# Expert slots in twos: a 64-row remainder of the down projection in two row tiles

## The chip, the cores and the metric

The kernel runs on one core of a Trainium2 chip. The metric is the device time of one execution in microseconds (us). Engines are named as the profile names them: PE is TensorE (matmuls and transposes), PEld its weight loads, DVE is VectorE, ACT is ScalarE, POOL is GpSimd, SP is SyncE, which here only issues transfers.

## The reference, cut to what matters

A cross-attention layer is followed by a mixture-of-experts feed-forward layer over 4096 tokens of width D = 256. The change touches only the routed experts. Each token goes to the 2 best of E = 8 experts, each expert having a hidden width of F = 192:

```python
h = jax.nn.silu(jnp.einsum('nd,edf->enf', xr, Wg)) * jnp.einsum('nd,edf->enf', xr, Wu)
out_all = jnp.einsum('enf,efd->end', h, Wd)
routed = out_all[exp, jnp.arange(exp.shape[0])]
out = shared.at[tok].add(routed * w[:, None])
```

All arithmetic of this part is in float32.

## The kernel before, in words

The first two thirds of the kernel compute attention, routing and the shared expert. Tokens are sorted by expert into DRAM (`sorted_rows`), in tiles of 128 rows that belong to one expert. There are 72 such tiles, called slots, and they are worked in 18 turns of four: the first turn and the last are written out, and a hardware loop (`quads`) runs the sixteen between. The number of a slot's expert is read from a table (`etile`) into a register, which then selects the weights.

For one slot, PE does the following. It transposes the 128 x 256 rows (`transposes`, L944, two slots to a call). It multiplies them with gate and up weights, 384 columns in two chunks of 128 rows (`up`, L955). ACT takes the silu of the gate half (L705), and DVE multiplies it with the up half (L1402, `inner`). PE transposes the product, 192 columns as two pieces of 96 (`turn`, L962), DVE copies it out of PSUM (L1408, `columns`), and PE does the down projection as two chunks of 96 rows and 256 columns (`down`, L971). DVE scales the result by the router's weight (L1417, `result`). POOL adds it to the output in DRAM with an indirect transfer (L530, a scatter), and it has a buffer for each of the four slots of a turn. `columns` in the ACT program (L696) copies the transposed rows of the next turn, two slots at a time.

The order of PE within a turn is written out by hand: up 0, up 1, turn 0, up 2, turn 1, down 0, up 3, turn 2, down 1, transposes of the next turn's first half, turn 3, down 2, transposes of its second half, down 3. That of DVE is: inner 0, inner 1, columns 0, inner 2, columns 1, result 0, inner 3, columns 2, result 1, columns 3, result 2, `places` of the next turn (small table operations, L1387 to L1394), result 3. Gate banks and down banks are two each, by k % 2.

POOL waits before the scatter of slot i for the scatter three before it; where a slot is the first tile of an expert it also waits until the scatter of the slot before has landed, and one further where it is among the first two, since two experts may hold the same token. These last waits use values that it loads from a table (L527).

The shared expert has the same width, 192. Its down projection (`shared_down`) runs for each pair of token tiles two matmuls over the full 128 rows (L1019) and then two over 64 rows, one in the lower half of the array and one in the upper (L1022). The helper `aside` increments a semaphore of its own.

A float32 matmul stands in the trace as two MATMUL records (and two LDWEIGHTS), a float32 transpose as one.

Of the kernel before, what the change touches and what calls it, by code (L numbers as in the profile page):

```python
# [22 lines left out]
ALU = mybir.AluOpType  # L23
# [52 lines left out]
def more(a, tiles):  # L76

    return not (isinstance(a, int) and a == tiles // 4 - 1)


def build(nc, x, xT, ctxT, wq, wkv, wp, bp, ln_g, ln_b, centre, ident, ident16, own, wr, wgu, wd, wgu_s, wd_s, e_bias, tri_c, rev_c, reg_c, tok_c, tst_c, fill_c,
          gate_c, x2_cols, sorted_rows, out):
    ctx = ExitStack()
    with ctx:
# [6 lines left out]
        def sem(name):  # L91
            return ctx.enter_context(nc.semaphore(name))

        def views(memory, *shapes):

            at, out_ = 0, []
            for shape in shapes:
                n_ = int(np.prod(shape))
                v_ = memory[:, at:at + n_]
                if len(shape) == 2:  # L100
                    v_ = v_.rearrange("p (a b) -> p a b", a=shape[0])
                if len(shape) == 3:
                    v_ = v_.rearrange("p (a b c) -> p a b c", a=shape[0], b=shape[1])
                out_.append(v_)
                at += n_
            return out_
# [70 lines left out]
        gate = gate.bitcast(I32)  # L177
        spare_at = spare_at.bitcast(I32)
        xs_col, hs0, hs1, gs0, gs1 = views(scores_in[:, :], (2, 4, D), (2, 4, P), (2, 2, P), (4, P), (4, P))
        x_col, act_g, h_in, h_col = views(scores_in[:, :], (4, D), (4, F), (2, F), (4, D))  # L180
        x_row, y_out = views(VS[:, :, :, :].rearrange("p b h d -> p (b h d)"), (4, ROW), (4, D)) if False else (
            views(VS[:, :, :, :].rearrange("p b h d -> p (b h d)"), (4, ROW))[0], VR[:, :, :, :].rearrange("p b g d -> p (b g) d").rearrange(
                "p (k q) d -> p k (q d)", k=4))
# [97 lines left out]
        f_xt, f_xc, f_gu, f_si, f_h, f_ht, f_hc, f_y, f_yd = (  # L281
            {k: sem(f"{k}_{n_}") for k in kinds_} for n_ in ("xt", "xc", "gu", "si", "h", "ht", "hc", "y", "yd"))
        e_dst = sem("e_dst")
        e_chain = sem("e_chain")
        y_st = [sem(f"y_st{i}") for i in range(4)]
        spare_set = sem("spare_set")

        def gate_bank(k):

            return bankS[:, k % 2, :]  # L290

        def down_bank(k):
            return bankS[:, 2 + k % 2, 0:D]
# [9 lines left out]
        def aside(eng):  # L303

            eng.sem_inc(aside_n[eng.engine], 1)
# [11 lines left out]
        def _(sp):  # L317
# [32 lines left out]
            sp.wait_ge(kt_rd, len(halves))  # L350
            for k in range(KC):
                sp.dma_start(wgu_sb[:, k], wgu[k * P:(k + 1) * P]).then_inc(w_in, 16)
            for k in range(FC):
                sp.dma_start(wd_sb[0:FP, k], wd[k * FP:(k + 1) * FP]).then_inc(w_in, 16)
            for m in range(LATE):
                store(m)

# [176 lines left out]
        def _(act):  # L534
# [156 lines left out]
            def columns(a):  # L691


                for h in range(2):
                    act.wait_ge(f_xt["e"], 2 * a + (h + 1))
                    act.activation(x_col[:, 2 * h:2 * h + 2], row_bank(h).rearrange("p (t c) -> p t c", t=2), ACT.Copy) \  # L696
                        .then_inc(f_xc["e"], 1)

            def ffn(kind, tiles):
                def gates(a):  # L700
                    for k in range(4):
                        act.wait_ge(f_gu[kind], 4 * a + (k + 1))
                        if not isinstance(a, int) or a >= 1:
                            act.wait_ge(f_h[kind], 4 * a + (k - 3))
                        act.activation(act_g[:, k], gate_bank(k)[:, 0:F], ACT.Silu).then_inc(f_si[kind], 1)  # L705
                    if more(a, tiles):
                        columns(a + 1)
                return gates

            def shared(a):  # L710

                act.wait_ge(s_gu, 3 * a + 1)
                if a >= 1:
                    act.wait_ge(s_h, 2 * a - 1)
                act.activation(gs0, bankS[:, 0, :], ACT.Silu).then_inc(s_si, 1)
                act.wait_ge(s_gu, 3 * a + 3)
                if a >= 1:
                    act.wait_ge(s_h, 2 * a)
                act.activation(gs1[0:P // 2], bankS[0:P // 2, 2, :], ACT.Silu).then_inc(s_si, 1)
# [8 lines left out]
            logit_exps(PARTS - 1)  # L728
            for a in range(1, QUADS):
                shared(a)  # L730
            columns(0)
            quads(act, SLOTS, ffn("e", SLOTS))

        @block.tensor
        def _(pe):
# [211 lines left out]
            def ffn(kind, tiles):  # L947
                def four(a):
                    def up(k, e_):

                        if k % 2 == 0:
                            pe.wait_ge(f_xc["e"], 2 * a + (k // 2 + 1))
                        for c in range(KC):
                            rhs = wgu_sb[:, c, ds(e_, 1), :].rearrange("p o f -> p (o f)")
                            last = pe.matmul(gate_bank(k)[:, 0:2 * F], x_col[:, k, c * P:(c + 1) * P], rhs, start=(c == 0), stop=(c == KC - 1))  # L955
                        last.then_inc(f_gu[kind], 1)

                    def turn(k):

                        pe.wait_ge(f_h[kind], 4 * a + (k + 1))  # L960
                        for c in range(FC):
                            last = pe.transpose((bankQ, bankR)[k % 2][0:FP, c * P:(c + 1) * P], h_in[:, k % 2, c * FP:(c + 1) * FP], id32[:, :])  # L962
                        last.then_inc(f_ht[kind], 1)

                    def down(k, e_):
                        pe.wait_ge(f_hc[kind], 4 * a + (k + 1))
                        if k >= 2 or not isinstance(a, int) or a >= 1:
                            pe.wait_ge(f_yd[kind], 4 * a + (k - 1))
                        for c in range(FC):
                            rhs = wd_sb[0:FP, c, ds(e_, 1), :].rearrange("p o d -> p (o d)")  # L970
                            last = pe.matmul(down_bank(k), h_col[0:FP, k, c * P:(c + 1) * P], rhs,  # L971
                                             start=(c == 0), stop=(c == FC - 1))
                        last.then_inc(f_y[kind], 1)

                    e_ = [expert(4 * a)] + [None] * 3
                    for k in range(4):
                        up(k, e_[k])
                        if k < 3:
                            e_[k + 1] = expert(4 * a + (k + 1))
                        if k >= 1:  # L980
                            turn(k - 1)
                        if k >= 2:
                            down(k - 2, e_[k - 2])
                    if more(a, tiles):
                        transposes(a + 1, 0)
                    turn(3)
                    down(2, e_[2])
                    if more(a, tiles):
                        transposes(a + 1, 1)
                    down(3, e_[3])  # L990
                return four

            pe.wait_ge(ws_in, 16 * 2)
# [50 lines left out]
            for a in range(3, QUADS):  # L1044
                shared(a)
            shared_down(QUADS - 1)
            pe.wait_ge(w_in, 16 * (KC + FC))
            pe.wait_ge(routed, 1)
            transposes(0, 0)
            transposes(0, 1)  # L1050
# [3 lines left out]
        def _(dve):  # L1054
# [341 lines left out]
            def ffn(kind, tiles):  # L1396
                def four(a):
                    def inner(k):
                        dve.wait_ge(f_si[kind], 4 * a + (k + 1))
                        if k >= 2 or not isinstance(a, int) or a >= 1:  # L1400
                            dve.wait_ge(f_ht[kind], 4 * a + (k - 1))
                        dve.tensor_tensor(h_in[:, k % 2], act_g[:, k], gate_bank(k)[:, F:2 * F], ALU.mult).then_inc(f_h[kind], 1)  # L1402

                    def columns(k):

                        dve.wait_ge(f_ht[kind], 4 * a + (k + 1))
                        aside(dve)
                        dve.tensor_copy(h_col[0:FP, k], (bankQ, bankR)[k % 2][0:FP, 0:D]).then_inc(f_hc[kind], 1)  # L1408

                    def result(k):  # L1410
                        dve.wait_ge(f_y[kind], 4 * a + (k + 1))
                        if not isinstance(a, int) or a >= 1:
                            dve.wait_ge(y_st[k], BASE + 16 * a)
                        dve.wait_ge(e_dst, 2 * a + (k // 2 + 1))
                        aside(dve)
                        w_k = w_slot[:, ds(4 * a + k, 1)]
                        dve.tensor_tensor(y_out[:, k], down_bank(k), w_k.to_broadcast([P, D]), ALU.mult).then_inc(f_yd[kind], 1)  # L1417

                    inner(0)
                    inner(1)  # L1420
                    columns(0)
                    inner(2)
                    columns(1)
                    result(0)
                    inner(3)
                    columns(2)
                    result(1)
                    columns(3)
                    result(2)
                    if more(a, tiles):  # L1430
                        places(a + 1)
                    result(3)
                return four

# [98 lines left out]
```

## Time and profile before

| | |
|---|---|
| median of 3 runs | 616.65 us (615.98 to 617.1) |
| the profiled execution's own time | 616.69 us |
| its span in the profile | 614.9 us |
| PE busy | 524.6 us, 85% of the span |
| DVE busy | 345.0 us, 56% |
| ACT busy | 239.4 us, 39% |
| POOL busy | 244.2 us, 40% |

The expert slots run from about 405 us to the end of the span. Busy shares say little on their own here, since every stage has another limit; the stage of the slots is to be read by itself, from the order of the instructions in one turn.

### The profile page before, as it was taken

What the parts mean: (1) busy time and instruction counts of PE and PEld (TensorE: products, weight loads), DVE (VectorE), ACT (ScalarE), POOL (GpSimd) and SP (SyncE); (2) the same over time, 40 slices, a digit from 0 to 9 for tenths busy, and PEclk for the clock granted to TensorE, in tenths of its full rate; (3) what the DMA queues carried; (4) which work ended last, traced back from release to release, by engine and by line L of the source; (5) the groups of instructions that cost most, each with busy time, mean ns of one, the idle gap of its engine ahead of it and who ended that gap; (6) DMA issues with size and microseconds to landing.
All of it is one profiled execution on the core that took longest, in us unless ns stands there. A gap on an engine that the chain in (4) does not pass through costs nothing.

```text
span 614.9 us, 10970 instructions
## 1 busy us (share of the span) xinstructions
PE 524.6 (85%) x2868; PEld 311.6 (51%) x2869; DVE 345.0 (56%) x1040; ACT 239.4 (39%) x468; POOL 244.2 (40%) x218
## 2 busy tenths in 40 slices
PE   4746899998798977988689999479999999999990
PEld 3633245544354444433265555157676766767670
DVE  5875556777747757635556663225555555555550
ACT  0256888776647834654324111012222222222220
POOL 5353411120011533442114475605656547564644
PEclk9956999998969967988879999879999999999996
DMA  8903701110011211121054384225656547565634
GB/s 276 354 30 132 212 18 36 45 61 18 17 36 35 88 52 53 60 80 52 19 190 150 105 275 155 91 73 80 116 84 105 99 80 118 86 110 88 103 55 48
DMA packets 41685, 59.75 MB, mean 97 GB/s; under 512 B 6703, under 2 KB 32047, under 8 KB 41168
## 3 DMA queue, kind: packets, MB, share of 16 engines
q0 software_dynamic: 16256, 26.49, 21.2%
q1 hardware_dynamic: 25392, 32.82, 17.9%
q8 instruction: 17, 0.28, 0.2%
q14 instruction: 20, 0.16, 0.1%
HBM read 31.76 MB, written 29.52 MB: 100 GB/s over the span
## 4 chain that ended last, share of the span: by engine, by line
PE 67%; DVE 13%; DMA 7%; issue 5%; ACT 4%; POOL 2%; POOLq 1%; SPq 1%; DVEq 0%; ACTq 0%
PE bankS L955 13%; PE bankS L971 8%; PE bankV L866 7%; PE bankR L741 7%; PE bankS L1006 6%; PE bankQ L741 5%; DMA out<-VR,attn 5%; PE bankV L870 3%; PE bankS L841 2%; PE bankS L853 2%; PE bankR L748 1%; ACT attn L622 1%; PE bankS L1022 1%; PE bankD L944 1%; PE bankQ L962 1%
## 5 line engine op out<-in xcount | busy, mean ns | idle before, releaser
L530 POOL DMA_INDIRECT out<-VR,attn x72 | 111.1, 1544 | 101.2 <-DVE VR L1417 57.0
L955 PE MATMUL bankS<-experts,scores_in 128*128 x288 | 105.0, 498 | 2.1 <-issue 1.1
L473 POOL DMA_INDIRECT sorted_rows<-XR,route x64 | 63.3, 989 | 107.1 <-PE bankD L872 48.6
L622 ACT ACTIVATE attn<-bankS,bias 128x512 f32<-128x512 f32 x128 | 81.1, 680 | 24.3 <-PE bankS L841 24.2
L971 PE MATMUL bankS<-experts,scores_in 96*128 x288 | 74.3, 380 | 0.0
L866 PE MATMUL bankV<-attn,VS 128*32 128x512 f32 x256 | 69.0, 664 | 1.7 <-DVE OTT L1192 1.7
L955 PEld LDWEIGHTS bankS<-experts,scores_in 128*128 128x128 f32 x288 | 52.6, 193 | 34.2 <-issue 9.7
L868 PE MATMUL bankD<-attn,ON 128*32 128x512 f32 x256 | 68.9, 664 | 0.0
L705 ACT ACTIVATE scores_in<-bankS 128x192 f32<-128x192 f32 x72 | 23.8, 330 | 110.8 <-PE bankS L955 110.8
L409 POOL DMA_DIRECT2D x_in<-in_xT x13 | 9.6, 736 | 127.3 <-PE bankQ L741 126.3
L1402 DVE TENSOR_TENSOR scores_in<-scores_in,bankS 128x192 f32<-128x192 f32 x72 | 25.5, 354 | 52.5 <-ACT scores_in L705 52.1
L971 PEld LDWEIGHTS bankS<-experts,scores_in 96*128 96x128 f32 x288 | 48.9, 190 | 4.6 <-issue 0.7
L1417 DVE TENSOR_TENSOR VR<-bankS,attn 128x256 f32<-128x256 f32 x72 | 30.6, 425 | 29.0 <-PE bankS L971 14.6
L1006 PE MATMUL bankS<-scores_in,wgus_sb 128*128 128x512 f32 x96 | 43.8, 603 | 0.0
L741 PE MATMUL bankQ<-wq_sb,x_in 128*128 128x256 f32 x112 | 35.0, 470 | 0.0
L870 PE MATMUL bankV<-attn,VR 128*32 128x512 f32 x128 | 34.7, 621 | 0.0
L872 PE MATMUL bankD<-attn,OR 128*32 128x512 f32 x128 | 34.6, 621 | 0.0
L748 PE MATMUL bankR<-id,XR 128*128 128x128 f32 x56 | 10.7, 323 | 27.3 <-DVE XR L1213 27.3
L866 PEld LDWEIGHTS bankV<-attn,VS 128*32 128x32 f32 x256 | 13.0, 117 | 39.9 <-issue 33.9
L1199 DVE TENSOR_TENSOR X<-X,bankR 128x512 f32<-128x512 f32 x14 | 9.6, 688 | 38.3 <-PE bankR L741 38.3
L741 PEld LDWEIGHTS bankQ<-wq_sb,x_in 128*128 128x128 f32 x112 | 26.0, 241 | 4.8 <-issue 0.3
L1006 PEld LDWEIGHTS bankS<-scores_in,wgus_sb 128*128 128x128 f32 x96 | 17.5, 190 | 20.7 <-issue 20.1
(252 smaller groups left out, 916.9 us busy)
## 6 DMA issues: line engine op xcount, KB each, us to landing
VS<-sorted_rows SPq DMA_DIRECT2D x72, 130.0 KB, 2.9
x_cols<-X2T SPq DMA_DIRECT2D x16, 256.0 KB, 2.0
scores_in<-x_cols SPq DMA_DIRECT2D x16, 256.0 KB, 2.8
out<-X POOLq DMA_DIRECT2D x8, 512.0 KB, 4.1
x_in<-in_xT POOLq DMA_DIRECT2D x15, 256.0 KB, 3.5
experts<-in_wgu SPq DMA_DIRECT2D x2, 1536.0 KB, 9.1
X<-in_x SPq DMA_DIRECT2D x1, 2048.0 KB, 16.2
experts<-in_wd SPq DMA_DIRECT2D x2, 768.0 KB, 15.9
```

Of the source, the lines that this page charges most:

```text
L473: pool.indirect_dma_start(sorted_rows.rearrange("s p r -> (s p) r"), bass.IndirectOffsetOnAxis(ap=index, axis=0), rows, None, bounds_check ...
L530: pool.indirect_dma_start(out, bass.IndirectOffsetOnAxis(ap=dest[:, i:i + 1], axis=0), y_out[:, i % 4], None, bounds_check=B * N + SPARE - ...
L622: act.activation(Pb[:, u % 2, c, :], bankS[:, c % GH, :], ACT.Exp, bias=bias[:, b, GH * g + c:GH * g + c + 1] if c < GH else biasR[:, b, g ...
L741: last = pe.matmul(bank[:, t * width:(t + 1) * width], columns(t, k), weights[:, k, :], start=(k == 0), stop=(k == KC - 1))
L866: pe.matmul(bankV[v_at:v_at + 32, :], VS[:, b, GH * g + 2 * c + a_, :], Pb[:, u % 2, 2 * c + a_, :], start=(a_ == 0), stop=False)
L868: pe.matmul(bankD[d_at:d_at + 32, :], ON[:, a_, :], Pb[:, u % 2, 2 * c + a_, :], start=(a_ == 0), stop=False)
L870: pe.matmul(bankV[v_at:v_at + 32, :], VR[:, b, g, 32 * c:32 * c + 32], Pb[:, u % 2, GH, :], start=False, stop=True)
L872: last = pe.matmul(bankD[d_at:d_at + 32, :], ones_r[:, 32 * c:32 * c + 32], Pb[:, u % 2, GH, :], start=False, stop=True)
L955: last = pe.matmul(gate_bank(k)[:, 0:2 * F], x_col[:, k, c * P:(c + 1) * P], rhs, start=(c == 0), stop=(c == KC - 1))
L971: last = pe.matmul(down_bank(k), h_col[0:FP, k, c * P:(c + 1) * P], rhs, start=(c == 0), stop=(c == FC - 1))
L1006: last = pe.matmul(bankS[:, c, :], wgus_sb[:, k, c * P:(c + 1) * P], xs_col[:, a % 2, :, k * P:(k + 1) * P], start=(k == 0), stop=(k == KC ...
L1417: dve.tensor_tensor(y_out[:, k], down_bank(k), w_k.to_broadcast([P, D]), ALU.mult).then_inc(f_yd[kind], 1)
```

## The change

Slots are worked in twos, h = 0 and 1 in a turn. The product of a pair is transposed in three pieces of 128 columns in place of four of 96: the first 128 hidden columns of either slot, and a third piece that holds the last 64 of both. For that DVE writes the product of an odd slot with its two parts exchanged, in two multiplications (64 and 128 columns) in place of one. One copy of 128 x 384 then takes the place of two of 96 x 256. `down` works a pair: two matmuls over 128 rows, one for each slot, and then two over 64 rows, one slot in the lower half of the array and the other in the upper. The 64 weight rows of the remainder are loaded twice, once for either half of the partitions, and as the two experts may differ, ACT copies each slot's 64 x 256 weights into `wd_rest`, with a load of the expert number ahead of each copy. The orders of PE and DVE within a turn are new, as the diff shows.

```diff
+            sp.dma_start(wd_sb[:, 0], wd[0:P]).then_inc(w_in, 16)
+            for r in range(2):
+                sp.dma_start(wd_sb[r * P // 2:(r + 1) * P // 2, 1], wd[P:F]).then_inc(w_in, 16)
...
+            def rest_weights(a, k):
+                h, rows = k // 2, slice(P // 2 * (k % 2), P // 2 * (k % 2) + P // 2)
+                if not isinstance(a, int) or a >= 1:
+                    act.wait_ge(f_y["e"], 2 * a + (h - 1))
+                    aside(act)
+                e_ = act.value_load(etile[0:1, ds(4 * a + k, 1)], min_val=0, max_val=E - 1)
+                act.activation(wd_rest[rows, h], wd_sb[rows, 1, ds(e_, 1), :].rearrange("p o d -> p (o d)"), ACT.Copy).then_inc(f_wr, 1)
...
                         act.activation(act_g[:, k], gate_bank(k)[:, 0:F], ACT.Silu).then_inc(f_si[kind], 1)
+                        rest_weights(a, k)
...
+                    def turn(h):
+                        bank = (bankQ, bankR)[h]
+                        pe.wait_ge(f_h[kind], 4 * a + (2 * h + 2))
+                        for t in range(2):
+                            pe.transpose(bank[:, t * P:(t + 1) * P], h_in[:, h, 2 * P * t:2 * P * t + P], id32[:, :])
+                        pe.transpose(bank[:, 2 * P:3 * P], h_in[:, h, P:2 * P], id32[:, :]).then_inc(f_ht[kind], 1)
+
+                    def down(h, e_):
+                        half = P // 2
+                        pe.wait_ge(f_hc[kind], 2 * a + (h + 1))
+                        pe.wait_ge(f_wr, 4 * a + (2 * h + 2))
+                        if h >= 1 or not isinstance(a, int) or a >= 1:
+                            pe.wait_ge(f_yd[kind], 4 * a + 2 * h)
+                        for t in range(2):
+                            rhs = wd_sb[:, 0, ds(e_[t], 1), :].rearrange("p o d -> p (o d)")
+                            pe.matmul(down_bank(t), h_col[:, h, t * P:(t + 1) * P], rhs, start=True, stop=False)
+                        for t in range(2):
+                            rows = slice(half * t, half * t + half)
+                            last = pe.matmul(down_bank(t), h_col[rows, h, 2 * P:3 * P], wd_rest[rows, h], start=False, stop=True)
                         last.then_inc(f_y[kind], 1)
...
                     for k in range(4):
+                        if k >= 2:
+                            pe.wait_ge(f_h[kind], 4 * a + (k - 1))
                         up(k, e_[k])
                         if k < 3:
                             e_[k + 1] = expert(4 * a + (k + 1))
-                        if k >= 1:
-                            turn(k - 1)
-                        if k >= 2:
-                            down(k - 2, e_[k - 2])
+                        if k == 2:
+                            turn(0)
+                    down(0, e_[0:2])
                     if more(a, tiles):
                         transposes(a + 1, 0)
-                    turn(3)
-                    down(2, e_[2])
+                    turn(1)
                     if more(a, tiles):
                         transposes(a + 1, 1)
-                    down(3, e_[3])
+                    down(1, e_[2:4])
...
+                        if k % 2 == 0:
+                            last = dve.tensor_tensor(h_in[:, k // 2, 0:F], act_g[:, k], gate_bank(k)[:, F:2 * F], ALU.mult)
+                        else:
+                            dve.tensor_tensor(h_in[:, k // 2, F:2 * P], act_g[:, k, P:F], gate_bank(k)[:, F + P:2 * F], ALU.mult)
+                            last = dve.tensor_tensor(h_in[:, k // 2, 2 * P:2 * F], act_g[:, k, 0:P], gate_bank(k)[:, F:F + P], ALU.mult)
...
+                        dve.tensor_copy(h_col[:, h], (bankQ, bankR)[h][:, 0:2 * F]).then_inc(f_hc[kind], 1)
...
                     inner(1)
                     columns(0)
                     inner(2)
+                    inner(3)
+                    result(0)
+                    result(1)
                     columns(1)
-                    result(0)
-                    inner(3)
-                    columns(2)
-                    result(1)
-                    columns(3)
-                    result(2)
                     if more(a, tiles):
                         places(a + 1)
+                    result(2)
                     result(3)
```

## Rows read from the trace of the kernel before

**Rows 1.** Busy time by stretch (windows): turns 0 to 13, turns 14 to 17; busy PE, PEld, DVE, ACT, POOL, clock
```profile
405.50:558.20 152.70, 150.81 (x673) 105.19 (x672) 80.84 (x301) 35.80 (x85) 81.98 (x54) 0.99 0.57 94
558.20:600.30 42.10, 41.80 (x184) 28.95 (x184) 22.19 (x83) 8.87 (x22) 22.91 (x15) 1.00 0.56 85
```

**Rows 2.** Timeline of PE, turn 5: start us, length us, engine, line, count
```profile
460.71 2.84 PE L955 MATMUL bankS<-experts,scores_in 128*128 x8
463.39 0.38 PE L962 MATMUL bankQ<-id,scores_in 128*96 128x128 f32 x2
463.61 1.46 PE L955 MATMUL bankS<-experts,scores_in 128*128 x4
...
469.02 1.03 PE L971 MATMUL bankS<-experts,scores_in 96*128 x4
469.89 0.60 PE L944 MATMUL bankD<-id,VS 128*128 128x128 f32 x4
470.32 1.03 PE L971 MATMUL bankS<-experts,scores_in 96*128 x4
471.44 0.58 PE L955 MATMUL bankS<-experts,scores_in 128*128 x1
```

**Rows 3.** Timeline of the shared expert's down projection, 364.7 to 370.5 us
```profile
365.23 0.59 PE L1019 MATMUL bankQ<-wds_sb,scores_in 128*128 128x256 f32 x2
...
365.75 0.48 PE L1022 MATMUL bankS<-wds_sb,scores_in 64*128 64x256 f32 x1
...
365.76 0.48 PE L1022 MATMUL bankQ<-wds_sb,scores_in 64*128 64x256 f32 x1
...
366.08 0.38 PE L1022 MATMUL bankQ<-wds_sb,scores_in 64*128 64x256 f32 x1
366.38 0.30 PEld L1019 LDWEIGHTS bankS<-wds_sb,scores_in 128*128 128x128 f32 x2 [0.33 <-issue]
...
367.44 0.48 PE L1022 MATMUL bankS<-wds_sb,scores_in 64*128 64x256 f32 x1
```

**Rows 4.** Groups by shape: busy us, mean ns of one, idle before
```profile
L1449 DVE TENSOR_TENSOR scores_in<-scores_in,bankS 128x512 f32<-128x512 f32 x8 | 5.5, 688 | 6.7 <-PE bankS L1006 5.4 <-ACT scores_in L715 1.2
L1408 DVE COPY scores_in<-bankQ 96x256 f32<-96x256 f32 x36 | 14.8, 412 | 0.0
L556 ACT ACTIVATE qs<-nq 128x512 f16<-128x512 f32 x16 | 10.1, 629 | 3.5 <-DVE nq L1118 3.5
```

**Rows 5.** Timeline from a product to its transpose (turn 9), and of a result (turn 14)
```profile
505.95 0.35 DVE L1402 TENSOR_TENSOR scores_in<-scores_in,bankS 128x192 f32<-128x192 f32 x1 [0.46 <-ACT scores_in L705]
506.36 0.28 PEld L962 LDWEIGHTS bankQ<-id,scores_in 128*96 128x96 f32 x2 [0.30 <-DVE scores_in L1402]
506.51 0.38 PE L962 MATMUL bankQ<-id,scores_in 128*96 128x128 f32 x2
...
562.63 1.03 PE L971 MATMUL bankS<-experts,scores_in 96*128 x4
562.69 0.33 ACT L705 ACTIVATE scores_in<-bankS 128x192 f32<-128x192 f32 x1 [1.18 <-PE bankS L955]
...
564.12 0.43 DVE L1417 TENSOR_TENSOR VR<-bankS,attn 128x256 f32<-128x256 f32 x1 [0.38 <-issue]
```

**Rows 6.** Timeline of POOL: slots 63, 64, 65 and 71
```profile
583.80 1.54 POOL L530 DMA_INDIRECT out<-VR,attn  x1 [0.63 <-DMA out<-VR,attn]
589.24 1.54 POOL L530 DMA_INDIRECT out<-VR,attn  x1 [3.90 <-issue]
594.47 1.54 POOL L530 DMA_INDIRECT out<-VR,attn  x1 [3.68 <-issue]
...
607.59 1.54 POOL L530 DMA_INDIRECT out<-VR,attn  x1 [0.67 <-issue]
```

**Rows 7.** The chain that ended last: one register load of POOL
```profile
593.08 0.29 POOLq L527
```

**Rows 8.** Timeline of PE: the start of turn 15
```profile
568.95 1.23 PE L955 MATMUL bankS<-experts,scores_in 128*128 x3
```

More of the change, by code:

```diff
@@ L179, in build @@
         xs_col, hs0, hs1, gs0, gs1 = views(scores_in[:, :], (2, 4, D), (2, 4, P), (2, 2, P), (4, P), (4, P))
-        x_col, act_g, h_in, h_col = views(scores_in[:, :], (4, D), (4, F), (2, F), (4, D))
+        x_col, act_g, h_in, h_col, wd_rest = views(scores_in[:, :], (4, D), (4, F), (2, 2 * F), (2, 2 * F), (2, D))
         x_row, y_out = views(VS[:, :, :, :].rearrange("p b h d -> p (b h d)"), (4, ROW), (4, D)) if False else (
@@ L283, in build @@
         e_dst = sem("e_dst")
+        f_wr = sem("f_wr")
         e_chain = sem("e_chain")
@@ L352, in _ @@
                 sp.dma_start(wgu_sb[:, k], wgu[k * P:(k + 1) * P]).then_inc(w_in, 16)
-            for k in range(FC):
-                sp.dma_start(wd_sb[0:FP, k], wd[k * FP:(k + 1) * FP]).then_inc(w_in, 16)
+            sp.dma_start(wd_sb[:, 0], wd[0:P]).then_inc(w_in, 16)
+            for r in range(2):
+                sp.dma_start(wd_sb[r * P // 2:(r + 1) * P // 2, 1], wd[P:F]).then_inc(w_in, 16)
             for m in range(LATE):
@@ L730, in _ @@
                 shared(a)
+            act.wait_ge(routed, 1)
+            act.wait_ge(w_in, 16 * (KC + 3))
             columns(0)
@@ L956, in up @@
                         last.then_inc(f_gu[kind], 1)
[L958 to L972, printed above, removed]
+                    def turn(h):
[16 more added lines that the diff above has]
+                            last = pe.matmul(down_bank(t), h_col[rows, h, 2 * P:3 * P], wd_rest[rows, h], start=False, stop=True)
                         last.then_inc(f_y[kind], 1)
@@ L1046, in _ @@
             shared_down(QUADS - 1)
-            pe.wait_ge(w_in, 16 * (KC + FC))
+            pe.wait_ge(w_in, 16 * (KC + 3))
             pe.wait_ge(routed, 1)
@@ L1399, in inner, with columns @@
                         dve.wait_ge(f_si[kind], 4 * a + (k + 1))
[L1400 to L1406, printed above, removed]
+                        if not isinstance(a, int) or a >= 1:
+                            dve.wait_ge(f_ht[kind], 2 * a + (k // 2 - 1))
+                        if k % 2 == 0:
[3 more added lines that the diff above has]
+                            last = dve.tensor_tensor(h_in[:, k // 2, 2 * P:2 * F], act_g[:, k, 0:P], gate_bank(k)[:, F:F + P], ALU.mult)
+                        last.then_inc(f_h[kind], 1)
+                    def columns(h):
+                        dve.wait_ge(f_ht[kind], 2 * a + (h + 1))
                         aside(dve)
-                        dve.tensor_copy(h_col[0:FP, k], (bankQ, bankR)[k % 2][0:FP, 0:D]).then_inc(f_hc[kind], 1)
+                        dve.tensor_copy(h_col[:, h], (bankQ, bankR)[h][:, 0:2 * F]).then_inc(f_hc[kind], 1)
                     def result(k):
-                        dve.wait_ge(f_y[kind], 4 * a + (k + 1))
+                        dve.wait_ge(f_y[kind], 2 * a + (k // 2 + 1))
                         if not isinstance(a, int) or a >= 1:
```

## The prediction

> **What bounds the kernel now.** I read the busy times by stretch first. From 405.5 to 600.3 us PE is busy for all but 2.2 us of 194.8, at a granted clock of 0.99 to 1.00 (the 2.4 GHz level), while DVE and POOL are busy about half the time and ACT a quarter [rows 1]. After that PE has nothing to do and POOL scatters on. So there are two clocks to watch: PE's period per turn, and POOL's chain at the end.
>
> The timeline of a turn gives the period: 471.44 - 460.71 = 10.73 us. Starts inside it give the pieces, better than the lengths, which contain the way through the array: `up` is 8 records from 460.71 to 463.39 less the late first start, that is 1.29 us for one slot; `turn` 0.22 (463.39 to 463.61); four row transposes 0.43 to 0.44 (469.89 to 470.32), 0.109 each; one `down` 0.87 (469.02 to 469.89), 0.216 for each record [rows 2]. Sum: 4 x 1.29 + 4 x 0.865 + 4 x 0.22 + 2 x 0.44 = 10.37. The other 0.36 is the loop's own turn: the last `down` starts at 470.32 and has streamed by 471.19, and the next weight load comes only at 471.4. Everything else is back to back.
>
> At the end, slot 63 is scattered at 583.80, 14.85 us after turn 15 began (568.95) [rows 6, 8]. Slots 64 and 65 are first tiles and wait for landings (5.44 and 5.23 us after the one before), then six scatters follow every 2.19 us, up to 607.59; the span ends 7.3 us later [rows 6]. From slot 63 on, 31.1 us are POOL's and not PE's. So PE's period counts for the 15 turns ahead of turn 15 and not for the last three, unless it becomes a good deal worse: PE was done at 600.3 against the last scatter at 607.59.
>
> **The change part by part, per turn.**
>
> *Full chunks and fewer transposes.* Two pairs, each with four full records of 0.216 (0.865) and, were the row tiles free, two more lengths for the four half-height records (0.43): 2 x 1.295 = 2.59 in place of 3.46. Six transposes of 0.109 = 0.655 in place of 0.88. Ideal: 5.16 + 2.59 + 0.655 + 0.88 + 0.36 = 9.64, a gain of 1.09.
>
> *What the row tiles really cost.* The shared expert does exactly this pair. The two halves do run together (365.75 and 365.76). But the first half-height record starts 0.52 after a full one whose successor should be done after 0.43, the second pair comes 0.32 after the first, and the next full load waits until 366.38, with 0.33 us of idle before it, put down to issue. From 365.75 to the same place at 367.44 is 1.69 us, against 1.295 of streaming [rows 3]. So 0.40 is lost in each trip into the row tiles and back, 0.80 per turn. The second way back falls into the loop's 0.36, so I take 0.6; ends 0.4 and 0.8. The Trainium skill, "TensorEngine Tiling (Array Packing)", Key Properties, says that changing the tiling mode drains TensorE, and gives up to 2x for a contraction of 64 rows or less. The trace agrees with the first (the 0.40), and with the second only inside the mode; by the 2x alone the sum would have nothing in this place.
>
> *The wait in front of the second `down`.* Before, a copy of columns had a whole `down` and four transposes to hide behind (turn 3, down 2, transposes, down 3). Now turn(1) is followed by 0.44 of transposes and then by down(1), which needs columns(1). That copy stands on DVE behind result(0) and result(1), which wait for down(0). Time from down(0)'s first record: last record ends 0.96 + 0.32 + 0.38 = 1.67. A result starts 0.46 after its `down` ended (562.63 + 1.03 to 564.12 [rows 5]); I have it start at 2.05. Two results of 0.43 [rows 5] with a little overlap end at 2.87. The copy of 384 columns lies halfway between 0.412 for 256 and 0.688 for 512, the nearest DVE rows that read PSUM at those widths: 0.55 [rows 4], to 3.42. From the end of a DVE product (506.30) to the transpose that needs it (506.51) it is 0.21, weight load included [rows 5]: 3.6. PE itself is free at 1.70 + 0.44 + 0.33 + 0.44 = 2.91. Stall 0.7; with the result starting 0.15 earlier and tighter overlap 0.45. I take 0.6; ends 0.4 and 0.9. Nothing covers it: PE has no other work queued.
>
> *Others.* DVE's odd products become 64 and 128 columns: by the same slope, 1.08 ns a column, from the 0.35 of 192 [rows 5], 0.21 + 0.28, about 0.1 more than one of 192. That lies in slack: `up` 2 runs ahead of turn(0) for 1.29 us, and the product of slot 1 is ready some 1.1 us after up 1 (silu 0.33, product 0.45, hand-overs). The third product has down(0) ahead of turn(1). `up` 2 now waits for product 0 as turn(0) did, at the same moment: nothing. POOL still gets four results a turn, now in twos; it needs 4 x 2.19 = 8.8 us for them, under the period, and result 0 comes later in the turn but result 3 earlier against POOL's queue, so slot 63 stays within 0.3 us of 14.85.
>
> *ACT's copies.* 64 x 256 lies between the silu's 0.33 for 192 columns and 0.629 for 512, that is about 0.39 [rows 4, 5]. Silu 0.33, a register load (POOL's takes 0.29 [rows 7]) and copy are 1.01 of the 1.29 between two silus: hidden, as ACT idles 1.18 ahead of each. Queued behind a copy are the next silu and then the row columns of the next turn; if the load took 0.35 more, each silu would be late and turn(0) with it. Ends 0 and 0.35 per turn. Waits on f_y are for a turn ago, met long before. *The loads:* three of 1.0 MB and 2 x 0.5 MB in place of two of 0.75 MB, over 300 us before use; 0.5 MB more is about 3 us of transfer beside attention, cost nothing, at most 1. *The loop's turn:* the last gate, columns(1), now has sixteen PE instructions after it instead of eight, which can make the sequencer later at the loop's end; 0.05, ends -0.15 and 0.2.
>
> **Sum.** 9.64 + 0.6 + 0.6 + 0.05 = 10.89 us a turn against 10.73: +0.16. Fifteen turns: +2.4. Turn 5 stands for all of them: fifteen of 10.73 from turn 0's 405.5 give 566.5, and turn 15 began at 568.95 [rows 1, 8], so 2.5 us lie in the start and in single late turns, which I leave in both. 616.69 (the profiled execution; the median is 616.65) + 2.4 = 619.1.
>
> **The rivals.**
> - *Forecast, 619.1, chance 0.42.* The packing is paid back by the two trips and by the wait at down(1). Its own range is 617.9 to 623.
> - *Equal, 616.5, chance 0.23.* The same, with both terms at the low side (0.5 and 0.5): 10.69. What can be measured of this kernel is about 0.2%, 1.2 us, either way, from 615.4 to 617.9.
> - *Faster: PE's sequencer gains at the loop's turn and DVE's chain is short, 612, chance 0.17.* Down(1) leaves 1.3 us of queued work to cover the branch, so the 0.36 becomes the way back of 0.2; with a stall of 0.4: 9.64 - 0.36 + 0.2 + 0.6 + 0.4 = 10.48, -0.25 x 15 = -3.8, 612.9. By the whole 2x, with no trip cost, it is 9.64 + 0.6 = 10.24, -7.4, 609.3. For it: the first turn out of the loop has no such gap. Against it: 0.40 was lost each time in rows 3. It decides where trips and stall together stay under 1.09.
> - *Slower: ACT's loads and copies come into the silu chain, 624.5, chance 0.18.* +0.35 a turn more, x 15 = +5.3. For it: four register loads a turn in a queue that had none. Against it: 0.28 to spare. The same time comes out if a stall of 0.9 and trips of 0.8 hold (+0.5 a turn, +7.5, 626.6).
>
> Faster by over 0.2%: 0.19 (the third, and the edge of the second); within 0.2%: 0.23; slower: 0.58. The range leaves out one in ten on each side: 612.5 to 626.5.
>
> **What the changed profile would show.** The start-to-start of L955 after the loop's turn: 10.9, under 10.7 if faster. L1022's pattern in the down projection: half-height records in pairs 0.01 apart, with about 0.1 more in front, between and behind. An idle time of PEld ahead of the second pair's full matmuls, released by DVE's copy, of 0.5 to 0.7; none would make me wrong on the faster side. Silus 0.25 after their `up`, as now; later would be the ACT rival. POOL's last nine scatters unchanged in spacing, slot 63 some 14.6 after turn 15 starts. PE's clock 1.00 throughout; if the gaps lowered it, all of the sum would be off. Wrong, too, if POOL were late enough with its landings for result(0) and result(1) to wait for a buffer, since columns(1) now queues behind them; after the two first tiles at slots 31 and 32 that is nearest.

## The result, and the profile after

The changed kernel takes 620.73 us (median of 12 runs, 619.72 to 624.81) against 617.0 us (12 runs) of the kernel before on the same chips: ratio 1.0079, 95% interval 1.0057 to 1.010. It is slower by 0.8%: 3.7 us between the medians, 4.9 us by the ratio, where 619.1 (+2.4 us) and "slower" had been forecast. The profiled execution took 621.41 us, with a span of 619.6 us where that of before was 614.9. One execution among the experiments below (changed, loads ahead) took 771.44 us at a granted clock of 0.642, and its ratio leaves it out.

The head of the page of the changed kernel: span, then busy us, share and instructions of each engine.

```profile
span 619.6 us, 11251 instructions
PE 520.6 (84%) x2832; PEld 292.0 (47%) x2833; DVE 334.7 (54%) x1040; ACT 268.7 (43%) x541; POOL 244.2 (39%) x218
```

PE, its weight loads and DVE all have less to do than before (524.6, 311.6 and 345.0 us there), ACT 29 us more. With less work on the engine that was busy almost without a pause, the span is 4.7 us longer: what grew is waiting. PE's granted clock is 1.00 from turn 1 on, as before, so the clock has no part in it. The timeline of PE in turn 5 shows where, and answers to [rows 2].

```profile
461.31 4.28 PE L969 MATMUL bankS<-experts,scores_in 128*128 x12
465.43 0.38 PE L977 MATMUL bankQ<-id,scores_in 128*128 128x128 f32 x2
465.65 0.27 PE L978 MATMUL bankQ<-id,scores_in 128*128 128x128 f32 x1
465.75 1.46 PE L969 MATMUL bankS<-experts,scores_in 128*128 x4
467.05 1.03 PE L989 MATMUL bankS<-experts,scores_in 128*128 x4
468.00 0.70 PE L992 MATMUL bankS<-scores_in 64*128 64x256 f32 x4
468.64 0.66 PE L958 MATMUL bankV<-id,VS 128*128 128x128 f32 x4
469.13 0.38 PE L977 MATMUL bankR<-id,scores_in 128*128 128x128 f32 x2
469.35 0.27 PE L978 MATMUL bankR<-id,scores_in 128*128 128x128 f32 x1
469.46 0.60 PE L958 MATMUL bankD<-id,VS 128*128 128x128 f32 x4
470.51 1.12 PE L989 MATMUL bankS<-experts,scores_in 128*128 x4 [0.45 <-DVE scores_in L1433]
471.57 0.70 PE L992 MATMUL bankS<-scores_in 64*128 64x256 f32 x4
472.20 4.28 PE L969 MATMUL bankS<-experts,scores_in 128*128 x12
```

From 461.31 to 472.20 a turn takes 10.89 us, where it took 10.73. I read start to start. A record whose weights were not yet loaded is longer by about 0.1, and I count it as streaming from 0.11 after its start (461.42 for 461.31, 470.62 for 470.51, 472.31 for 472.20). Then the turn is made up so:

- First down projection, 467.05 to the second `turn` at 469.13, less 0.44 of row transposes: 1.64, of which 1.295 is streaming. The trip into the row tiles and back costs 0.35. The second down projection, 470.62 to 472.31, takes 1.69, so its trip costs 0.39.
- The last row transposes have streamed by 469.90 (469.46 and 0.44), and the second down projection streams from 470.62: for 0.72 PE streams nothing.
- The loop's own gap of 0.36 is gone: the way back from the row tiles is as long at the loop's turn (471.57 to 472.20) as in the middle of the turn (468.00 to 468.64).
- Three `up` take 465.43 - 461.42 = 4.01 where they stream 3.87: 0.14 in front of `up` 2.

9.28 (all the streaming) + 0.35 + 0.39 + 0.72 + 0.14 = 10.88.

What PE waits for is seen one turn earlier, in the timeline of all engines in turn 4. Its last row is results 2 and 3, which end at 462.45.

```profile
458.23 0.78 DVE L1442 TENSOR_TENSOR VR<-bankS,attn 128x256 f32<-128x256 f32 x2 [1.08 <-PE bankS L992]
...
458.92 0.55 DVE L1433 COPY scores_in<-bankR 128x384 f32<-128x384 f32 x1
...
459.62 1.13 PE L989 MATMUL bankS<-experts,scores_in 128*128 x4 [0.45 <-DVE scores_in L1433]
...
461.67 0.78 DVE L1442 TENSOR_TENSOR VR<-bankS,attn 128x256 f32<-128x256 f32 x2 [0.35 <-PE bankS L992]
```

Results 0 and 1, the copy of 384 columns, and then the matmul, with nothing idle between results and copy on DVE.

The other half of the loss is behind PE. Timeline of PE at the start of turn 15, and of POOL in the changed kernel (slots 60, 63, 64, 65 and 71):

```profile
572.04 4.28 PE L969 MATMUL bankS<-experts,scores_in 128*128 x12
```

```profile
582.34 1.54 POOL L532 DMA_INDIRECT out<-VR,attn  x1 [2.31 <-DMA out<-VR,attn]
...
588.65 1.54 POOL L532 DMA_INDIRECT out<-VR,attn  x1 [0.99 <-DMA out<-VR,attn]
593.96 1.54 POOL L532 DMA_INDIRECT out<-VR,attn  x1 [3.76 <-issue]
599.29 1.54 POOL L532 DMA_INDIRECT out<-VR,attn  x1 [3.79 <-issue]
...
612.42 1.54 POOL L532 DMA_INDIRECT out<-VR,attn  x1 [0.63 <-DMA out<-VR,attn]
```

For comparison, slot 60 in the kernel before:

```profile
577.42 1.54 POOL L530 DMA_INDIRECT out<-VR,attn  x1 [2.19 <-DMA out<-VR,attn]
```

From slot 63 to slot 71 it is 23.77 us, as before (23.79) [rows 6]. But slot 63 comes 16.61 us after turn 15 starts and not 14.85. Of the 4.85 us by which slot 63 is later, 1.76 arose here, 0.26 ahead of turn 1 (which starts at 417.71, before at 417.45), and 2.83 in the fourteen turns between.

Of these 2.83, turn 9 alone gives 1.09: it takes 12.59 us, and 11.50 before. The timeline of turn 9:

```profile
504.90 2.85 PE L969 MATMUL bankS<-experts,scores_in 128*128 x8
...
507.52 0.42 DVE L1442 TENSOR_TENSOR VR<-bankS,attn 128x256 f32<-128x256 f32 x1 [1.84 <-DMA out<-VR,attn]
...
508.14 0.35 DVE L1423 TENSOR_TENSOR scores_in<-scores_in,bankS 128x192 f32<-128x192 f32 x1 [0.19 <-issue]
...
508.73 1.55 PE L969 MATMUL bankS<-experts,scores_in 128*128 x4 [0.98 <-DVE scores_in L1423]
...
514.76 0.42 DVE L1442 TENSOR_TENSOR VR<-bankS,attn 128x256 f32<-128x256 f32 x1 [0.53 <-DMA out<-VR,attn]
...
515.10 0.55 DVE L1433 COPY scores_in<-bankR 128x384 f32<-128x384 f32 x1
...
515.80 1.13 PE L989 MATMUL bankS<-experts,scores_in 128*128 x4 [1.05 <-DVE scores_in L1433]
```

Result 3 of the turn before waits 1.84 us for the landing of the scatter that last used its buffer (slot 31, a first tile, scattered at 503.30). Product 0 stands behind it on DVE, and `up` 2 behind that: 1.10 us more than in a steady turn up to `turn` of the first pair. Later in the turn result 1 waits 0.53 us for a landing too, the copy stands behind it, and the second down projection waits 1.05 in place of 0.45: another 0.60. Together this is the 1.70 by which turn 9 exceeds 10.89.

### The profile page after: what moved, and what is told of

Same layout as the page of the kernel before. It is cut to its first block, busy times and chain, and to the rows that moved or that the text cites. A ratio compares the mean times of both kernels' runs of the same rounds, so it can differ in the third digit from the quotient of the medians.

```text
span 619.6 us, 11251 instructions
## 1 busy us (share of the span) xinstructions
PE 520.6 (84%) x2832; PEld 292.0 (47%) x2833; DVE 334.7 (54%) x1040; ACT 268.7 (43%) x541; POOL 244.2 (39%) x218
## 4 chain that ended last, share of the span: by engine, by line
PE 64%; DVE 14%; DMA 8%; issue 5%; ACT 4%; POOL 2%; POOLq 1%; SPq 1%; DVEq 0%; ACTq 0%
PE bankS L969 13%; PE bankV L880 7%; PE bankR L755 7%; PE bankS L1026 6%; DMA out<-VR,attn 6%; PE bankQ L755 5%; PE bankS L989 4%; PE bankV L884 3%; PE bankS L992 3%; PE bankS L855 2%; PE bankS L867 2%; ACT attn L624 2%; PE bankR L762 1%; PE bankS L1042 1%; DVE scores_in L1433 1%
## 5 line engine op out<-in xcount | busy, mean ns | idle before, releaser
L969 PE MATMUL bankS<-experts,scores_in 128*128 x288 | 104.8, 504 | 1.0 <-DVE scores_in L1423 1.0
L969 PEld LDWEIGHTS bankS<-experts,scores_in 128*128 128x128 f32 x288 | 51.3, 192 | 40.1 <-issue 16.5
L989 PE MATMUL bankS<-experts,scores_in 128*128 x144 | 38.7, 391 | 11.0 <-DVE scores_in L1433 11.0
L1442 DVE TENSOR_TENSOR VR<-bankS,attn 128x256 f32<-128x256 f32 x72 | 28.3, 425 | 32.0 <-PE bankS L992 22.6
L708 ACT ACTIVATE scores_in<-experts 64x256 f32 x72 | 29.9, 415 | 35.8 <-issue 35.8
L989 PEld LDWEIGHTS bankS<-experts,scores_in 128*128 128x128 f32 x144 | 25.8, 189 | 21.8 <-issue 18.5
L762 PE MATMUL bankR<-id,XR 128*128 128x128 f32 x56 | 10.7, 323 | 27.4 <-DVE XR L1233 27.4
```

Of the source, the lines that this page charges most:

```text
L708: act.activation(wd_rest[rows, h], wd_sb[rows, 1, ds(e_, 1), :].rearrange("p o d -> p (o d)"), ACT.Copy).then_inc(f_wr, 1)
L989: pe.matmul(down_bank(t), h_col[:, h, t * P:(t + 1) * P], rhs, start=True, stop=False)
```

## The experiments

Where a turn is given, it is the steady distance from one turn's first `up` to the next. "Offset" is the time from the start of turn 15 to the scatter of slot 63. Turn and offset are read from one profiled execution of each version, the ratio from all its runs.

| version | turn | turn 9 | offset | ratio to before (95%) |
|---|---|---|---|---|
| before | 10.73 | 11.50 | 14.85 | |
| changed | 10.89 | 12.59 | 16.61 | 1.0079 (1.0057 to 1.010) |
| other banks | 10.43 | 12.62 | 17.19 | 1.0007 (0.9995 to 1.0018) |
| changed, no copies by ACT | 10.89 | 13.04 | 17.18 | 1.0094 (1.0071 to 1.0117) |
| changed, full height | 11.14 | 13.07 | 17.09 | 1.0143 (1.0118 to 1.0168) |
| changed, copy first | 11.64 | 11.77 | 17.68 | 1.0275 (1.0252 to 1.0298) |
| before, scatters in twos | 10.72 | 13.87 | 17.19 | 1.0078 (1.0054 to 1.0101) |
| before, loads ahead | 10.85 | 11.03 | 13.86 | 0.9992 (0.9971 to 1.0014) |
| changed, loads ahead | 10.89 | 10.89 | 15.05 | 1.0006 (0.9987 to 1.0025) |
| other banks, loads ahead | 10.43 | 11.79 | 15.99 | 0.9941 (0.9918 to 0.9964) |
| the same, full height | 10.54 | 11.19 | 15.83 | 0.9921 (0.9894 to 0.9947) |

**Other banks: is the wait DVE's row of results and copy?**

```diff
         def down_bank(k):
-            return bankS[:, 2 + k % 2, 0:D]
+            return bankS[:, 2 + k % 2, 0:D] if k < 2 else (bankQ, bankR)[k - 2][:, 0:D]
...
                         pe.wait_ge(f_h[kind], 4 * a + (2 * h + 2))
+                        if h == 0 and (not isinstance(a, int) or a >= 1):
+                            pe.wait_ge(f_yd[kind], 4 * a)
...
-                        if h >= 1 or not isinstance(a, int) or a >= 1:
-                            pe.wait_ge(f_yd[kind], 4 * a + 2 * h)
-                            pe.matmul(down_bank(t), ...)
+                            pe.matmul(down_bank(2 * h + t), ...)
...
+                    turn(1)
                     if more(a, tiles):
                         transposes(a + 1, 0)
-                    turn(1)
...
                     inner(3)
+                    columns(1)
                     result(0)
                     result(1)
-                    columns(1)
```

The wait for `f_yd` that is added to the first `turn` keeps its transposes off a bank until the results of the turn before have been read from it.

> The changed kernel, with three edits that belong together: the second pair's down projection writes two other PSUM banks (those of the turned products), so that it needs no result of the first pair; DVE copies the second pair's columns ahead of results 0 and 1; PE turns the second pair ahead of both sets of row transposes. In the trace of the changed kernel the matmul of the second pair starts 0.72 us after PE ran dry, once a turn. My theory, that this wait is results and copy of the first and second pair standing in a row on DVE: columns start about 0.6 us after the first down projection ends, take 0.55, and PE has 1.3 us of other work, so that the wait falls to 0.1 to 0.2 and the turn from 10.89 to 10.3 or 10.4 us, 15 turns give 7 to 8 us, less about 0.7 because result 0 comes later: 612 to 614.5 us, faster than both. Rival, that the period is set by the switches into and out of the row tiles and by the order of PE: turn 10.8 to 10.9, 620 us. Rival, that POOL's scatters become the bound: turns of 10.4 but the end moves by under 2 us, 618 to 620.

Measured: 616.94 us, ratio 1.0007. The turn is 10.43, in the expected span. Timeline of this version, turn 12, from the second copy on:

```profile
542.97 0.56 DVE L1433 COPY scores_in<-bankR 128x384 f32<-128x384 f32 x1 [1.31 <-PE bankR L980]
543.09 0.60 PE L958 MATMUL bankD<-id,VS 128*128 128x128 f32 x4
...
543.45 0.74 DVE L1442 TENSOR_TENSOR VR<-bankS,attn 128x256 f32<-128x256 f32 x2
543.68 0.69 PE L989 MATMUL bankQ<-experts,scores_in 128*128 x2
...
545.37 1.88 PE L969 MATMUL bankS<-experts,scores_in 128*128 x5
546.20 1.54 POOL L532 DMA_INDIRECT out<-VR,attn  x1 [2.76 <-DMA out<-VR,attn]
```

The copy ends at 543.53, and the matmul that needs it streams from 543.79, 0.26 after the row transposes have: 9.28 + 0.35 + 0.39 + 0.14 + 0.26 = 10.42. So the wait of 0.72, now 0.26, was for the most part DVE's row of results and copy. But the total is that of before, and not 612 to 614.5; the rival on the scatters comes nearest to it, though its figure, 618 to 620, was too high. Turn 15 starts 2.68 us earlier than before (566.27), and slot 63 is scattered 0.34 earlier (583.46). The scatter of slot 48 comes 11.3 us after its turn began, since results 0 and 1 are now behind the copy and behind a longer turn, and turns 9 and 10 lost 3.1 us.

**Copy first, banks as they were.**

```diff
                     inner(3)
+                    columns(1)
                     result(0)
                     result(1)
-                    columns(1)
```

> The changed kernel with one edit: DVE copies the second pair's columns ahead of results 0 and 1; banks and PE's order stay. My theory of the wait at the second down projection: both the results of the first pair (its banks) and the columns are needed, and DVE does them one after the other, so their order is nothing: the turn stays at 10.8 to 11.0 us (a bit longer, since the copy starts only when the turn is done and the results follow), total 620 to 623. Rival, that only the copy's place behind the results matters: the turn falls to 10.4 to 10.5 and the total to 615 to 617, as with the other banks.

Measured: 633.29 us. Neither: the turn is 11.64, 0.75 longer.

```profile
472.36 0.56 DVE L1433 COPY scores_in<-bankR 128x384 f32<-128x384 f32 x1 [1.75 <-PE bankR L978]
...
472.84 0.75 DVE L1442 TENSOR_TENSOR VR<-bankS,attn 128x256 f32<-128x256 f32 x2
...
473.84 1.12 PE L989 MATMUL bankS<-experts,scores_in 128*128 x4 [1.20 <-DVE VR L1442]
```

The timeline of this version shows DVE idle for 1.75 us, with two results ready to be read behind it, until the turned columns come; then the down projection waits for the results, its banks. Both conditions hold, as I had written, but "the order is nothing" was wrong: the changed kernel fills the time until the columns are there with the results. It is the shared bank, together with the order, that has to go. PE's new order was not tried by itself; since the copy starts at once behind the results in the changed kernel (458.23 and 0.78, 458.92), earlier columns should not start it earlier, but that is argued.

**No copies by ACT.**

```diff
-                        rest_weights(a, k)
...
-                        pe.wait_ge(f_wr, 4 * a + (2 * h + 2))
-   ... wd_rest[rows, h], start=False, stop=True)
+   ... wd_sb[rows, 1, 0, :], start=False, stop=True)
```

> The changed kernel without ACT's register loads and copies of remainder weights: the 64-row matmuls read the weights of expert 0 in place, whatever the slot's expert (left out: the choice of the expert for the remainder). My theory, that ACT's copies lie in its idle time: turn 10.8 to 10.9 us, total within 1.5 us of the changed kernel's 620.7. Rival, that the loads and copies delay the silus and through them up 2 and the transposes: the 0.14 us that up 2 starts late in each turn goes, the turn is 10.7 to 10.75, total 618 to 618.5 or less.

Measured: 622.7 us (4 runs, 620.36 to 623.25), turn 10.89 as with the copies; the total is not lower without them, and its median is 2.0 us above that of the changed kernel, 0.5 more than I had allowed. The copies and loads cost PE nothing in a steady turn, and the 0.14 in front of `up` 2 is not theirs.

This run also says how far a single trace can be trusted. PE, DVE and POOL run the same orders as in the changed kernel, and yet its turn 9 takes 13.04 us against 12.59 and its offset is 17.18 against 16.61. Differences of about 0.5 us in these two columns have no meaning by themselves.

**Full height in place of the row tiles.**

```diff
-   ... h_col[rows, h, 2 * P:3 * P], wd_rest[rows, h], ...
+   ... h_col[:, h, 2 * P:3 * P], wd_rest[:, h], ...
```

> The changed kernel with the remainder as two matmuls over all 128 rows in place of two over 64 rows in two row tiles (the sums take in the other slot's rows too, so the remainder's share of the output is another one). It streams 0.43 us more for each pair and has no change of tiling. My theory, that a trip into the row tiles and back costs 0.35 to 0.40 us each: the pair takes 1.73 in place of 1.64 to 1.69, so the turn grows by 0.05 to 0.2 us only (more if the loop's own gap of up to 0.36 comes back at the turn's end), 11.0 to 11.3, total 622 to 626. Rival, that the row tiles gain their full 0.43 per pair and the loss is all elsewhere: the turn grows by 0.86 to 11.75 and the total by 13, to 634.

Measured: 624.18 us, turn 11.14. Timeline of PE, turn 5 of this version:

```profile
467.11 1.03 PE L992 MATMUL bankS<-scores_in 128*128 128x256 f32 x4
467.97 0.60 PE L958 MATMUL bankV<-id,VS 128*128 128x128 f32 x4
...
468.74 0.60 PE L958 MATMUL bankD<-id,VS 128*128 128x128 f32 x4
469.93 1.13 PE L989 MATMUL bankS<-experts,scores_in 128*128 x4 [0.59 <-DVE scores_in L1433]
470.89 1.03 PE L992 MATMUL bankS<-scores_in 128*128 128x256 f32 x4
471.76 0.49 PE L969 MATMUL bankS<-experts,scores_in 128*128 x1
```

Now the remainder's records follow each other at their streaming time (467.11 to 467.97 is 4 x 0.215), at the loop's turn too (0.87). The turn streams 0.86 more and is 0.25 longer: 0.86 more streaming, 0.74 of trips gone, and the wait in front of the second down projection longer by 0.14 (468.74 + 0.44 to 470.04 is 0.86) make +0.26. So the row tiles save 0.86 of streaming a turn and give 0.74 back. The Trainium skill, "TensorEngine Tiling (Array Packing)", Key Properties, has a drain at a change of mode. The trace agrees, with 0.35 to 0.39 us for a trip into the row tiles and back, against the 0.43 of streaming that a trip saves. (The "up to 2x" that the prediction names with it stands on that page under Theoretical Speedup.)

**Scatters in twos, on the kernel before.**

```diff
-                pool.wait_ge(f_yd["e"], i + 1)
+                pool.wait_ge(f_yd["e"], i // 2 * 2 + 2)
```

> The kernel before, with one edit: POOL waits before the scatters of a pair until both results are there. In the changed kernel turn 15 starts 3.1 us later than before, but the scatter of slot 63, from which on the end is fixed, comes 4.85 us later. My theory: POOL starts a turn's four scatters 2.1 us after its first result and needs 6.3 us for the rest, so the moment of the turn's first released scatter sets the last one; here turns stay at 10.73 us, the first release is 2.2 us later in the turn, and slot 63 and the end come about 2 us later: 618 to 619.5 us. Rival, that the last results of a turn set the scatter of slot 63: no change, 616 to 617.5.

Measured: 621.53 us, ratio 1.0078, more than I had expected. Timelines of this version: start of turn 15, and slots 60 and 63.

```profile
571.84 2.84 PE L955 MATMUL bankS<-experts,scores_in 128*128 x8
```

```profile
582.46 1.54 POOL L530 DMA_INDIRECT out<-VR,attn  x1 [2.19 <-DMA out<-VR,attn]
...
589.03 1.54 POOL L530 DMA_INDIRECT out<-VR,attn  x1 [0.60 <-DVE VR L1417]
```

The offset grew by 2.34, as foretold; 2.15 of it is there already at slot 60 (582.46 - 571.84 = 10.62, before 8.47). The rest is turns 9 and 10, 13.87 and 11.36 us: after the first tiles at slots 31 and 32 the scatters are late, results wait for their buffers, and PE with them. Later release alone, with PE's and DVE's programs untouched, costs as much as the whole change does. It is not the same release, though: here turn 9 loses 2.37 us to the kernel before and turn 10 another 0.64, and in the changed kernel turn 9 loses 1.09. The run shows that later release costs time in both places, and not how much of the changed kernel's loss it is.

**POOL's loads ahead of its waits, on both kernels and on the version with other banks.**

```diff
+                landed = [pool.value_load(gate[0:1, k, i:i + 1], ...) for k in range(min(i, 2))]
                 pool.wait_ge(f_yd["e"], i + 1)
                 if i >= 3:
                     pool.wait_ge(y_st[(i - 3) % 4], BASE + 16 * ((i - 3) // 4 + 1))
                 for k in range(min(i, 2)):
-                    landed = pool.value_load(gate[0:1, k, i:i + 1], ...)
-                    pool.wait_ge(y_st[(i - 1 - k) % 4], landed)
+                    pool.wait_ge(y_st[(i - 1 - k) % 4], landed[k])
```

> The kernel before, with one edit on POOL: the two register loads of each slot stand ahead of all its waits (for the result, for the scatter three before, for the landings) instead of between them. Theory that the scatters set the end: the time from a released result or a landed scatter to the next scatter falls by 0.6 to 1.2 us, which counts once for the first scatter of a turn and once each for the two first tiles at the end, and single late turns after slots 31 and 32 shrink: 2 to 3.5 us faster, 613 to 614.5. Rival, that PE's turns alone set the end: no change, 616 to 617.5.

Measured: 615.67 us (10 runs, 612.55 to 620.26), ratio 0.9992. That is less than expected. The offset fell by 0.99, but its steady turns vary between 10.7 and 10.9, for a reason that stays open; a gain can't be told from none.

> The changed kernel with the same edit on POOL. If 1.5 to 3 us of its loss against the kernel before came through later scatters, the edit gives it at least as much as it gives the kernel before, 2.5 to 4 us: 616.5 to 618, and turn 10 starts under 12 us after turn 9 in place of 12.6. Rival, PE alone: 620 to 621.

Measured: 617.67 us (10 runs, with the one of 771.44; 617.27 without it), ratio 1.0006 in place of 1.0079: the changed kernel gains 3 to 4.5 us, by medians or by ratios, and is level with the kernel before. Turn 9 is 10.89 like all others, the offset 15.05, and PE's program is the same. The last scatter is 3.43 us earlier (608.99 for 612.42): 1.13 by the start of turn 15, 1.56 by the offset, and 0.74 between slots 63 and 71 (23.03 for 23.77), where the first tiles 64 and 65 follow sooner too.

> The version with other banks for the second pair (turn 10.43 us, total equal to before) and the same edit on POOL. Theory: its turns had gained 0.3 us each, 2.7 us by turn 15, and later scatters took it back (slot 63 came 17.2 us after turn 15 started against 14.85). With a quicker POOL it keeps 3 to 5 us: 611.5 to 614, faster than the kernel before and at most equal to it with the same edit. Rival, that POOL's own rate, and not its latency, holds it at four scatters in 8.8 us plus a turn's waits: 615 to 617.

Measured: 611.85 us (6 runs, 610.95 to 614.56), ratio 0.9941: faster than both kernels, and than the one before by 0.6%. Its slot 63, on the timeline of POOL:

```profile
579.23 1.54 POOL L532 DMA_INDIRECT out<-VR,attn  x1 [0.51 <-DMA out<-VR,attn]
```

That is 4.57 us earlier than before (583.80) [rows 6].

**The last version at full height.** The edit is that of the first full-height run.

> The version with other banks and POOL's loads ahead (turn 10.43 us, 611.9 us), with the remainder as two matmuls over all 128 rows in place of two over 64 rows in two row tiles (the remainder's share of the output is another one). Theory from the first full-height run: two trips cost 0.74 us a turn and save 0.86 of streaming, so the row tiles are worth 0.1 to 0.15 us a turn once the wait at the second down projection is gone; turn 10.5 to 10.6, total 613 to 614.5. Rival, that they are worth the 0.25 us by which that run's turn was longer: 10.7, 615.5 to 616.

Measured: 611.91 us (5 runs), turn 10.54, 0.11 longer, as expected; the total is not longer, where 613 to 614.5 had been expected. Where DVE no longer makes PE wait, the row tiles give 0.11 us a turn on PE, and at the end of this kernel nothing that can be measured. A version of it that computes the reference would need weights that are zero in the other slot's rows, and was not built.

## Why the prediction was right, and where its terms were off

- **The turn.** 10.89 forecast, 10.89 measured, but by terms that cancel (-0.27, +0.12 and +0.14), which is luck. For the two trips and the loop's turn I had 0.6 + 0.36 + 0.05 = 1.01; they are 0.74, since each trip costs 0.35 to 0.39 and the loop's gap is gone altogether. It is gone with full height too, where the last down projection also has twice the records, so the part of the "faster" rival that rested on this held.
- **The wait at the second down projection.** 0.6 taken, 0.72 measured; its cause is shown by the other banks (0.26 left with them) and by copy first (longer). The chain is as reckoned: two results in 0.78, the copy in 0.55.
- **`up` 2.** "At the same moment: nothing" was wrong by 0.14. Its weight load starts 0.23 after product 0 is done (463.80 to 464.03), where the load of the transpose that waited there before took 0.06 [rows 5].

```profile
463.45 0.35 DVE L1423 TENSOR_TENSOR scores_in<-scores_in,bankS 128x192 f32<-128x192 f32 x1 [1.01 <-issue]
...
464.03 0.94 PEld L969 LDWEIGHTS bankS<-experts,scores_in 128*128 128x128 f32 x4 [0.49 <-issue]
```

  What the difference of 0.17 is, register arithmetic for the expert's weights behind the wait or something else, was only argued; that it isn't ACT's copies was shown.
- **ACT's copies, DVE's split product.** Hidden, as said; the copy takes 0.41 to 0.42 (0.39 taken), the copy of 384 columns 0.55 to 0.56 (0.55).
- **The step that was mis-sized: the offset of slot 63.** I had "within 0.3 us of 14.85"; it is 16.61. I wrote that result 3 comes earlier against POOL's queue, as if the last results counted. In the changed kernel they are done long before: results 2 and 3 of turn 4 end at 462.45, and slot 19 is scattered at 467.65. In the kernel before this could not be told: result 3 of turn 15 ends at 581.56, 2.24 ahead of slot 63, much as result 0 (575.26) is 2.16 ahead of slot 60.

```profile
467.65 1.54 POOL L532 DMA_INDIRECT out<-VR,attn  x1 [1.33 <-DMA out<-VR,attn]
```

  POOL starts a turn's scatters 2 to 3 us after result 0 and needs 6.3 to 6.4 us from the first to the fourth, before (577.42 to 583.80) and after (582.34 to 588.65). The fourth has to wait for the landing of the first, three before it, and a landing is what the trace names ahead of slot 63 in both kernels; that this wait makes the 6.3 was only argued. Result 0 moved from 6.3 us after the start of the turn (564.55 - 558.22) to about 8.2 (458.62 - 450.38). With turn 9, which the prediction named as the nearest danger without pricing it (1.09), this is 2.85 of the 4.85 us; the other 2.0 is what it had as 2.4. Scatters in twos on the kernel before showed both effects. POOL's loads ahead took turn 9 back entirely and 1.56 of the offset, but they take 0.99 off the offset of the kernel before too: between the two kernels with that edit, 1.19 of the 1.76 stays.
- **Two sums of the rivals.** 10.69 a turn gives 616.1 and not the 616.5 at the head of "equal", and "faster", headed 612, comes to 612.9. No chance hangs on either.

So the range held and so did the direction, with the mechanism on PE right. But 2.85 of the 4.85 us in the profiled executions, give or take the 0.5 us or so by which offset and turn 9 vary, came from a place that I had priced at nothing.

## What to carry to other kernels

Working two tiles as one halves the number of moments at which results are released: count what that does to the engine that sends them off, above all where it sets the end. A copy out of PSUM that had a whole matmul group to hide behind needs a new cover when groups are merged; here another bank together with another order took 0.46 of a wait of 0.72 away. Row tiles for two contractions of 64 rows are worth the streaming that they save less the change of mode on either side; with 256 float32 columns 0.11 us a turn was left here, and nothing in the total.

## What the runs showed of the hardware

- A trip into two row tiles and back to full height costs 0.35 to 0.39 us at a granted clock of 1.00, in the middle of a turn and at its end alike (0.40 in the shared expert [rows 3]); the two halves start 0.01 apart or less.
- The gap of 0.36 us at the turn of PE's hardware loop is there when eight loads and matmuls follow the last wait on another engine, and not in any version where sixteen do. That the longer queue covers the branch was only argued.
- POOL puts 2 to 3 us between the first released result of a turn and its scatter in this program. With its two register loads ahead of the waits the offset fell from 14.85 to 13.86 us on the kernel before, and from 16.61 to 15.05 on the changed one, each read from one execution.
